# Rotation of queries and keys in layer 0: from VectorE to GpSimd, by way of a ScalarE copy out of PSUM

## The reference, cut to what matters

```python
x = x + _L0_xattn_ref(_layernorm(x), ctx, 32, ...)   # top 32 of 257 keys
x = x + _L0_attn_ref(_layernorm(x), W_Q, W_K, W_V, W_O)
x = x + _L0_ffn_ref(_layernorm(x), ...)
...
def _L0_attn_ref(x, W_Q, W_K, W_V, W_O):             # 16 heads of 8
    q, k, v = proj(W_Q), proj(W_K), proj(W_V)
    q = q * cos + _rotate_half(q) * sin
    k = k * cos + _rotate_half(k) * sin
    attn = softmax(einsum('bhqd,bhkd->bhqk', q, k) / sqrt(8))
    return einsum('bld,ed->ble', merge(attn @ v), W_O)
```

## Time and profile before

| | |
|---|---|
| time, median of 3 runs | 1680.54 us (1679.21 to 1680.66) |
| the profiled execution | 1676.52 us, span 1674.7 us |
| VectorE busy over the span | 1084.9 us (65%) |
| TensorE matmul busy over the span | 1406.9 us (84%) |
| ScalarE busy | 809.1 us (48%) |
| GpSimd busy | 667.2 us (40%) |

### The profile page before, as it was taken

How to read it: one execution, slowest core, us unless ns; L and a number is a source line. 1 busy time by engine, 2 the same in 40 slices (tenths; PEclk the granted TensorE clock), 3 DMA queues, 4 the chain that set the end, 5 groups by cost and what they waited for, 6 DMA issues and landing times. The chain is left out here.

```text
span 1674.7 us, 44899 instructions
## 1 busy us (share of the span) xinstructions
PE 1406.9 (84%) x14646; PEld 1047.7 (63%) x14646; DVE 1084.9 (65%) x3491; ACT 809.1 (48%) x2363; POOL 667.2 (40%) x1261
## 2 busy tenths in 40 slices
PE   4888888866869979999999999979999999966774
PEld 2666666655557746666666666657777777755662
DVE  3888888856410057877877877756777777762224
ACT  2555555531223337777777777744344344412330
POOL 1444444420523424444444444432234344444553
PEclk9999999975779979999999999989999999987887
DMA  5555633300111132122122122100000000003224
GB/s 191 167 173 173 217 113 107 109 1 1 38 43 45 37 103 74 57 73 73 57 73 71 58 73 70 60 19 1 1 10 11 11 13 13 12 28 79 76 72 158
DMA packets 89364, 115.46 MB, mean 69 GB/s; under 512 B 12418, under 2 KB 68746, under 8 KB 89168
## 3 DMA queue, kind: packets, MB, share of 16 engines
q1 hardware_dynamic: 82608, 102.55, 19.3%
q0 software_dynamic: 6688, 12.07, 2.2%
HBM read 78.97 MB, written 37.32 MB: 69 GB/s over the span
## 5 line engine op out<-in xcount | busy, mean ns | idle before, releaser
L1658 ACT ACTIVATE c_pr<-c_pS,c_nm 128x257 f32<-128x257 f32 x512 | 238.4, 472 | 97.7 <-DVE c_nm L1794 97.7
L1794 DVE TENSOR_REDUCE c_nm<-c_pS 128x1 f32<-128x257 f32 (+1 forms) x384 | 173.2, 505 | 42.6 <-PE c_pS L1538 42.5
L2110 ACT ACTIVATE s_k<-s_pK 128x512 f32<-128x512 f32 x128 | 76.4, 597 | 179.2 <-PE s_pK L2007 177.7
L1542 PE MATMUL c_pT<-cst,c_pr 128*128 128x128 f32 x1024 | 162.9, 284 | 0.0
L2007 PE MATMUL s_pK<-s_hT,AH 128*128 128x128 f32 x1024 | 138.6, 285 | 0.5 <-ACT s_hT L2105 0.5
L2007 PEld LDWEIGHTS s_pK<-s_hT,AH 128*128 128x128 f32 x1024 | 125.0, 196 | 21.4 <-ACT s_k L2110 18.2
L1542 PEld LDWEIGHTS c_pT<-cst,c_pr 128*128 128x128 f32 x1024 | 111.3, 141 | 37.7 <-issue 37.7
L2028 PE MATMUL s_pM<-BH,s_uT 128*128 128x128 f32 x1024 | 123.8, 280 | 5.0 <-DVE LG L2259 5.0
L2028 PEld LDWEIGHTS s_pM<-BH,s_uT 128*128 128x128 f32 x1024 | 119.5, 196 | 7.7 <-DVE LG L2259 7.7
L1803 DVE COPY c_prT<-c_pT 128x512 f32<-128x512 f32 x128 | 88.5, 692 | 23.9 <-PE c_pT L1542 18.5
L1538 PE MATMUL c_pS<-c_ks,c_qq 32*128 32x257 f32 x1024 | 92.7, 431 | 13.1 <-POOL c_qq L1710 8.0
(11 more groups left out here) (354 smaller groups left out, 3343.4 us busy)
## 6 DMA issues: line engine op xcount, KB each, us to landing
rows_in<-c_blank SPq DMA_DIRECT2D x32, 520.0 KB, 3.1
a_ctxT<-in_ctxT SPq DMA_DIRECT2D x32, 514.0 KB, 3.5
c_ctxT<-in_ctxT SPq DMA_DIRECT2D x128, 128.5 KB
a_ctxN<-in_ctxR SPq DMA_DIRECT2D x32, 512.0 KB, 4.1
f_back<-rows_out SPq DMA_DIRECT2D x24, 256.0 KB, 6.2
f_hb<-rows_in SPq DMA_DIRECT2D x39, 130.0 KB
f_w<-in_f_w SPq DMA_DIRECT2D x16, 256.0 KB, 3.4
rows_in<-a_zero SPq DMA_DIRECT2D x7, 322.5 KB, 4.5
```

The source lines that it names most:

```text
L1542: mm = pe.transpose(pT[:, c, j, :], pr[:, b % 2, j, c * P:(c + 1) * P], k("ident"))
L1658: act.activation(pr[:, b % 2, c, :], pS[:, c, 0:S], ACT.Exp, bias=nm[:, c:c + 1], accum_out=den[:, b % 2, c:c + 1]).then_inc(e_ready.sem, 1)
L1794: dve.tensor_reduce(nm[:, c:end], pS[:, c:end, 0:S], AX.X, ALU.max, negate=True).then_inc(max_ready.sem, 1)
L2110: act.activation(k2[:, c * HK:(c + 1) * HK, :], pK[:, c % 2, :, :], ACT.Copy).then_inc(k_ready.sem, 1)
```

## The change

ScalarE gets a step `queries_keys`, behind `normed_x`: it copies the 512 columns of `pQ[:, 0, :]` into a new tile `flat` in SBUF. GpSimd gets `rotate`, which does the multiplication and the addition from `flat`, ahead of `spread_keys` and behind the first norm step; it waits for its own multiplication in between. VectorE loses both instructions. `add_bias` goes from second to last place in GpSimd's slot.

```diff
# ScalarE
+            def queries_keys(a):
+                act.wait_ge(qk_done.sem, qk_done.at(a))
+                if later(a):
+                    act.wait_ge(rot_ready.sem, rot_ready.at(a - 1))
+                act.activation(flat[:, :, :, :].rearrange("p c n t -> p (c n t)"), pQ[:, 0, :], ACT.Copy).then_inc(flat_ready.sem, 1)
...
                 run(normed_x, x)
+                run(queries_keys, a)
                 run(sums, u)
# GpSimd
+            def rotate(a):
+                pool.wait_ge(flat_ready.sem, flat_ready.at(a))
+                pool.tensor_tensor(rot[:, :, :, :], flat[:, :, :, :], k("rope")...broadcast_to([P, 2, 8, T]),
+                                   ALU.mult).then_inc(rot_ready.sem, 1)
+                pool.wait_ge(rot_ready.sem, rot_ready.at(a))
+                if later(a):
+                    pool.wait_ge(ss_done.sem, ss_done.at(a - 1))
+                pool.tensor_tensor(qk[...], rot[:, 0, :, :]..., rot[:, 1, :, :]..., ALU.add).then_inc(qk_ready.sem, 1)
...
                 run(lambda g: n1.gpsimd(pool, g), w_)
-                run(add_bias, x)
+                run(rotate, a)
                 run(spread_keys, a)
                 run(lambda g: n3.gpsimd(pool, g), z)
                 run(lambda g: n2.gpsimd(pool, g), u)
                 run(keep, z)
+                run(add_bias, x)
# VectorE
                 run(lambda u: sums_with_last(u, p, r), u)
-                run(rotate, a)
                 run(self_inverse_sums, z)
...
                 run(mark(2), t)
-                run(rotated, a)
                 run(largest(3), t)
```

More of the change, by code:

```diff
@@ L247, in attend_layer0 @@
         cs, cu, uT, vT = sb("cs", [P, D]), sb("u", [P, D]), sb("uT", [P, P]), sb("vT", [P, P])
-        hT2, rot, qk = sb("hT2", [P, P]), sb("rot", [P, 2, 8, T]), sb("qk", [P, 2, P])
+        hT2, flat, rot, qk = sb("hT2", [P, P]), sb("flat", [P, 2, 8, T]), sb("rot", [P, 2, 8, T]), sb("qk", [P, 2, P])
         kquad = sb("kquad", [P, BG, HQ, T])
@@ L286, in attend_layer0 @@
         h2T_done, h2T_ready = sig("h2T_done"), sig("h2T_ready")
-        qk_done, rot_ready, qk_ready, kq_ready = sig("qk_done"), sig("rot_ready"), sig("qk_ready"), sig("kq_ready")
+        qk_done, flat_ready, rot_ready, qk_ready, kq_ready = sig("qk_done"), sig("flat_ready"), sig("rot_ready"), sig("qk_ready"), sig("kq_ready")
         ss_done, smax_ready, sd_ready, se_ready = sig("ss_done"), sig("smax_ready"), sig("sd_ready"), sig("se_ready")
@@ L638, in add_bias @@
                                    bo0[:, :], ALU.add).then_inc(xb_ready.sem, 1)
+            def rotate(a):
+                pool.wait_ge(flat_ready.sem, flat_ready.at(a))
+                pool.tensor_tensor(rot[:, :, :, :], flat[:, :, :, :], k("rope").rearrange("p (c t) -> p c t", c=2).unsqueeze(2).broadcast_to([P, 2, 8, T]),
+                                   ALU.mult).then_inc(rot_ready.sem, 1)
+                pool.wait_ge(rot_ready.sem, rot_ready.at(a))
+                if later(a):
+                    pool.wait_ge(ss_done.sem, ss_done.at(a - 1))
+                pool.tensor_tensor(qk[:, :, :].rearrange("p a t -> p (a t)"), rot[:, 0, :, :].rearrange("p n t -> p (n t)"),
+                                   rot[:, 1, :, :].rearrange("p n t -> p (n t)"), ALU.add).then_inc(qk_ready.sem, 1)
             def spread_keys(a):
@@ L721, in rows_u @@
                 n2.vector_rows(dve, x_of(u))
[L723 to L732, removed]
             s4 = pQ[:, :, 0:P].rearrange("p c (h s) -> p c h s", h=HQ)
```

## The result

The changed kernel takes 1767.81 us (median of 4 runs, 1766.61 to 1770.07), the kernel before 1680.14 us (median of 4, 1679.21 to 1680.66). The ratio is 1.0525, with a 95% interval of 1.0509 to 1.0541: 88 us more. The forecast was 1747 with a range of 1703 to 1771. The time lies in the range, and it is that of the third rival, the low clock through all of the dense work.

The account below looks back on a forecast made before the run. VectorE looked like the bound, but the chain through GpSimd had only 0.27 us of slack. To the median 1680.5 us it added 27 for that chain and 41 for clock falls: 1748.5, stated as 1747, range 1703 to 1771.

Parts of the forecast that it names:

- the third rival: TensorE's clock stays low through all dense work in nearly every slot: 60 us in all, 1768 us; chance 0.20.
- That VectorE's busy share is no bound: VectorE is busy 89% of the stage's steady part, yet the chain through GpSimd, with 0.27 us slack, sets the slot.
- the fourth rival: VectorE is the bound and GpSimd's path hidden: at most 0.48 us less per slot, 1667 us; chance 0.05.
- ScalarE's copy costs nothing: ScalarE's copy of 512 columns from PSUM, 0.60 us, lies in 0.98 us of idle time and delays nothing.
- The chain through GpSimd, 0.92 us in a slot: From GpSimd's norm through kquad to VectorE's maxima: kquad ends 1.19 us later, less 0.27 slack, so 0.92 per slot.
- the sum of 27 us for the stage: GpSimd's longer path: 25.8 us over slots 3 to 30 plus 1.6 us in the last two slots.
- One short clock fall in each slot, 41 us: TensorE's clock falls on the dense work after the slot's start, 1.46 us in each of 28 slots.
- the upper bound: TensorE's clock low through all of its dense work, 2.16 us in each of 28 slots, 60 us.
- The idle time of TensorE before its scores: TensorE would stand idle 1.5 us before self_scores, where it was 0.34, in the slot's thinnest part.
- L217 behind GpSimd's product: VectorE's scaling waits behind GpSimd's multiplication for shared SBUF ports, some 0.9 us against 0.39, covered by the wait for kquad.

Follow-up runs that it names:

- VectorE's work put back: Changed kernel, but VectorE rotates again from ScalarE's copy while GpSimd repeats both products into unread tiles: 1769.84 us, 1.0555 against the kernel before.
- the kernel with seven matmuls: Changed kernel plus unread constant matmuls on TensorE in each slot, five ahead of self_scores and two behind scores: 1699.76 us, 1.0151 against the kernel before.
- with five matmuls: Changed kernel plus five unread constant matmuls on TensorE ahead of self_scores in each slot: 1719.46 us, 1.0264 against the kernel before.
- the full table: Changed kernel with rope spread once into a plain tile of 512 columns for GpSimd's multiplication: 1766.08 us, 1.0546 against the kernel before.

## Why the prediction was right in its mechanism and low in its time

**That VectorE's busy share is no bound.** Right: VectorE waits for TensorE ahead of `cs` and ahead of the maxima, and the fourth rival never came near. That the kernel with VectorE's work put back runs as the change does is weaker evidence than it looks, as both keep the falls' distance of 13.65 us.

**ScalarE's copy costs nothing.** Right: 0.60 us in idle time, and 1.002 when tried alone.

**The chain through GpSimd, 0.92 us in a slot.** Right in its links, low by 0.26. `rstd` took 0.55, `qk` 0.72 and `kquad` 1.04, as costed, but `rot` 1.27 and not 1.04. From `cs` to the maxima it was 5.31 us before and is 6.40 now, 1.09 more; where the clock is full the slot grew by 1.18. 0.23 of the missing 0.26 is the one product that I priced by `kquad` and L1721, which aren't of its kind. That the sum of 27 us for the stage nevertheless agrees with the 25 measured (28.7 by the traces) is partly luck: the kernel with seven matmuls also lacks the falls at 58.05 and 346.61 that the kernel before had the earlier trace rows.

**One short clock fall in each slot, 41 us.** That a fall comes in each slot was right (27 of the 28; the kernel before already had the first of them, at 58.05), its size was not, and this is the step that made the time 21 us too low. I priced it by the slot from 58.05 (1.46 us) and kept the one from 346.61 (2.16 us) as the upper bound. The changed kernel has 2.21 by the place of `cs`, 2.20 by the slots with and without falls, 63 us in all. What was wrong is where the fall begins: not just behind the slot's start, as at 58.05, but up to 1.7 us ahead of it, in the thin work, so that the low stretch is 6.8 us and not 3.4 and covers all of the dense products. It is not that a fall which recurs is a long one: the kernel before had a lone long one, and with five matmuls the nine falls of the looped slots were all short. I had named this as the third rival, with the right price, the right reason (the stretch begins with thin work) and a chance of 0.20.

**The idle time of TensorE before its scores.** Foreseen 1.5 us, measured 1.68. It is what brings the clock down: with work in that place, and the same wait on VectorE, the clock fell in nine looped slots in place of all 26, and only by short falls; with two more matmuls behind the cross scores it stayed up. By the rule of the Trainium skill that the prediction quotes (TensorE: Matmul & The Clock Gate, section "Why this matters for your kernels") a gap of this size is harmless. The trace doesn't agree: no wait for `kquad` was longer than 2.2 us, and the low clock cost 63 us.

**L217 behind GpSimd's product.** 1.20 us where 0.39 stood, and it ends at 220.89 with `rot`, at 220.81. Covered, as I said, by the wait for `kquad`. That the same lock costs 37 us where nothing covers it I hadn't seen: I took the bias's move to be harmless, and alone it isn't.

**What stays open.** The slot settles at 13.6 to 13.7 us in three kernels that differ on VectorE and GpSimd (the change, the full table, VectorE's work put back). The falls had that distance first and the slots followed; why the falls come 13.65 us apart no run shows, and none set the slot's length by itself. The 63 us are thus what this rhythm costs these kernels, not a sum of independent falls. How much of the change's loss is due to the bias's place wasn't tried either, since in the change `rot` has taken the place behind `rstd`.

## What to carry to other kernels

Before work goes from a busy engine to an idle one, find the one wait that its idle time consists of: if the moved work lands behind that wait, on the path to the engine that sets the end, it adds its duration, less the slack and what leaves the path, however idle the engine is. Then look first at what could let that wait end earlier; here moving one small VectorE instruction was worth 5%. Price a clock fall by where it begins: one that sets in during the thin work ahead of the dense work cost about 2.2 us here, one that set in about the slot's start, with the dense work, 1.3 to 1.6. And price an operation by rows of the same size and the same access pattern.

## What the runs showed of the hardware that I had not expected

- GpSimd's two-input float32 instructions took 0.45, 0.72 and 1.27 us for 128, 256 and 512 columns; with a factor repeated along the innermost elements 512 columns took 1.04 to 1.075.
- Which of two instructions starts first decides what the shared access to SBUF costs: L217 takes 0.34 us when it starts ahead of GpSimd's `kquad` and 0.97 when it starts 0.14 behind it. Through slots and clock together this was worth 35 us in one kernel (1710.43 against 1675.56).
- The granted clock fell for 3.4 us or for 6.8 us in this stage, by where in the slot it began to, and in three kernels the falls came 13.65 us apart while the first of these slots were still 13.8 to 14.1 us long.
- The clock needs no idle engine to be at the low level half of the time: TensorE's idle time before its self scores had a mean of 45.6 / 26 = 1.75 us, at a busy share of 80%.
- Ten matmul passes without use, 1.36 us of them in a slot, made the kernel faster by 2.5% (1.0264 against 1.0525), and with four more by 3.6%.
